# A layer on one core: from tile 4 on GpSimd makes the MLP's read instead of TensorE

## The chip, the cores and the metric

The kernel runs on one core of a Trainium2 chip. The time is the device time of one execution in microseconds; the number that counts is the median of the runs. All data is float32.

## The reference, cut to what matters

```python
def rat_read(res, W, gamma, beta, num_outputs):      # W is (512, outputs, 4)
    x = res.reshape(b, l, H, C)                      # H = 512, C = 4: 2048 values a row
    y = jnp.einsum('blhc,hoc->bloh', x, W)           # four neighbours make one value per output
    mu, var = y.mean(-1, keepdims=True), y.var(-1, keepdims=True)
    yn = (y - mu) * jax.lax.rsqrt(var + EPS)
    return (yn * gamma + beta).reshape(b, l, num_outputs * H)
...
qkv_in = rat_read(hidden_states, attn_read_w, ..., 3)
attn_out = attention(qkv_in, qkv_w, position_ids)            # causal, 16 heads
hidden_states = rat_write(hidden_states, attn_out, ...)      # the attention write
mlp_in = rat_read(hidden_states, mlp_read_w, ..., 2)         # the MLP's read
mlp_out = jax.nn.silu(gate(mlp_in[..., :H])) * up(mlp_in[..., H:])
hidden_states = rat_write(hidden_states, mlp_out, ...)       # the MLP write
...
x = x + layer(layernorm(x))
x = x + experts(layernorm(x))      # 8 experts of rank 16, weighed by a softmax router
```

`rat_write` makes from a projection of its input a new hidden state `hs * A_full + out * B_full`, elementwise over 2048 values a row, where `A_full` comes from exponentials of an outer product. x has 2 x 1024 rows of 2048 values.

## The kernel before

The 2048 rows are 16 tiles of 128 rows (one row a partition) and 4 blocks of 4 tiles. The program has three phases: the attention's reads and projections (`project_*`), the attention itself with the splitting of the MLP's weights on GpSimd (`attend_*`), and a mix of everything after (`mix_*`). Tiles 0 to 3 get their attention write partly during attention. All DMAs of the mix go out from one queue, SyncE's.

In the mix the work is made of small parts, each with a place on a common axis in which one MLP matmul step has length 1 and a block 64. The table `PLACES` gives the places: `a` is a tile's attention write and read, `w` its MLP write, `e` its expert, `t` the turn of a block, `h` the split of the MLP's middle, `m` the matmul steps. The list is sorted by place once, and each engine walks it in that order and does its share of each part; between engines only semaphores count. An engine never overtakes: what stands behind a waiting part waits too.

The parts of a tile `a`, i from 4 on, all on lane 0 (buffers `m_hs0`, `m_A0`): `load` of x into `m_hs0`, `wod` (16 matmuls, L1824), `low` and `delta` (L1838, L1845), `gates` (VectorE L1983 to L1998, among them the outer product L1992 into `m_A0`), `scale` (L2007, L2011, L2018, and on ScalarE L2213, L2217), `sum` (L2021, L2023, L2028, L2033, each over 1536 elements a partition). After the sum `m_hs0` holds the hidden state. Then comes the read: four `turn` parts, each with four 128x128 transposes on TensorE (L1809) and a copy from PSUM by ScalarE (L2183), and four `read` parts, each with four matmuls against `m_read2` (L1864; the profile has two records for each), which leave y in two PSUM banks. `stats` takes mean and variance on VectorE from PSUM (L2075, L2079, L2081) and a power on GpSimd (L2341); `norm` writes the normed y to `m_y0` to `m_y3` on ScalarE (L2241). The store of `m_hs0` to memory is issued by the queue at the place of `turn0`.

When a block's four tiles are there, the turn (`t`, TensorE L1908, VectorE L2130, ScalarE L2284, GpSimd L2353) makes the operand of its 32 matmul steps into the MLP (L1921, 12 matmuls each, a `m_win` weight load of 512 KB) and 32 steps out of it (L1933, `m_wods`, 316 KB). There are five weight buffers, and the load for step n + 5 is issued when step n is done. VectorE multiplies the middle (L2145) and splits it (L2159). The MLP write `w` of a tile runs the same instructions as `a` on lane 1 and ends with `x` (L2068, 2048 elements), on which the expert's first transpose (L1809 again) and its moments (ScalarE L2256, GpSimd L2347, L2349) wait. In blocks 1 and 2 the tiles `a` of the next block and `w` and `e` of the last one alternate.

In the profile, names stand without buffer numbers: `m_hs` is any of `m_hs0` to `m_hs2`.

## Time and profile before

| | |
|---|---|
| median of 3 runs | 1634.19 us (1629.28 to 1638.53) |
| profiled execution, span from first to last instruction | 1627.3 us |
| TensorE busy | 1531.8 us, 94% |
| VectorE busy | 1129.6 us, 69% |
| ScalarE busy | 921.9 us, 57% |
| GpSimd busy | 364.1 us, 22% |
| DMA queue of SyncE, share of 16 engines | 68.7% |
| blocks 0, 1, 2, 3 of the MLP | about 692 to 890, 894 to 1131, 1133 to 1358, 1359 to 1565 us |

Busy time is the time in which an engine runs at least one instruction. TensorE's groups share the time in which instructions overlap, so that a group's busy time is less than its count times its mean duration. For the profiled execution the page gives the span and no separate total; the median lies 6.9 us above the span.

### The profile page before, as it was taken

What the parts mean: (1) busy time and instruction counts of PE and PEld (TensorE: products, weight loads), DVE (VectorE), ACT (ScalarE), POOL (GpSimd) and SP (SyncE); (2) the same over time, 40 slices, a digit from 0 to 9 for tenths busy, and PEclk for the clock granted to TensorE, in tenths of its full rate; (3) what the DMA queues carried; (4) which work ended last, traced back from release to release, by engine and by line L of the source; (5) the groups of instructions that cost most, each with busy time, mean ns of one, the idle gap of its engine ahead of it and who ended that gap; (6) DMA issues with size and microseconds to landing.
All of it is one profiled execution on the core that took longest, in us unless ns stands there. A gap on an engine that the chain in (4) does not pass through costs nothing.

```text
span 1627.3 us, 25328 instructions
## 1 busy us (share of the span) xinstructions
PE 1531.8 (94%) x9574; PEld 1169.6 (72%) x9574; DVE 1129.6 (69%) x1782; ACT 921.9 (57%) x1702; POOL 364.1 (22%) x346
## 2 busy tenths in 40 slices
PE   7999999999999988899999999899999999999986
PEld 6567666666666656778798778798877898875554
DVE  7777745888888878644463785974776955636777
ACT  5444345888888776455543656643657644552443
POOL 1645555555433420110002000012000011001000
PEclk8999999999999999899999999999999999999998
DMA  9667677999987945356577766667766667756542
GB/s 371 204 254 243 223 181 229 276 293 284 273 233 197 253 138 189 130 185 223 202 218 233 258 226 221 214 218 232 265 233 221 223 197 237 218 180 213 203 178 104
DMA packets 127609, 360.94 MB, mean 222 GB/s; under 512 B 15744, under 2 KB 45056, under 8 KB 111872
## 3 DMA queue, kind: packets, MB, share of 16 engines
q1 hardware_dynamic: 127200, 359.19, 68.7%
q8 instruction: 76, 1.25, 0.3%
q14 instruction: 45, 0.37, 0.1%
q10 hardware_dynamic: 288, 0.13, 0.0%
HBM read 273.15 MB, written 86.11 MB: 221 GB/s over the span
## 4 chain that ended last, share of the span: by engine, by line
PE 74%; DVE 12%; ACT 6%; DMA 3%; issue 3%; POOL 1%; SPq 0%; DVEq 0%; ACTq 0%; POOLq 0%
PE ps L1921 21%; PE ps L1933 9%; PE ps L693 5%; PE ps L1249 5%; PE ps L1236 4%; PE ps L1272 4%; PE ps L1946 4%; PE ps L1879 3%; PE ps L1864 3%; PE ps L1809 3%; ACT a_p L1378 3%; PE ps L1824 3%; PE ps L1891 3%; DMA p_x<-in_x 2%; PE ps L652 2%
## 5 line engine op out<-in xcount | busy, mean ns | idle before, releaser
L1921 PE MATMUL ps<-m_y_split,m_win 128*128 128x512 f32 x1536 | 372.7, 396 | 2.7 <-issue 2.7
L1921 PEld LDWEIGHTS ps<-m_y_split,m_win 128*128 128x128 f32 x1536 | 284.2, 189 | 63.9 <-issue 7.1
L1308 DVE TENSOR_REDUCE a_negmax<-ps 128x1 f32<-128x640 f32 (+7 forms) x176 | 180.7, 1027 | 61.1 <-PE ps L1239 60.3
L1378 ACT ACTIVATE a_p<-ps,a_negmax 128x128 f32<-128x128 f32 (+7 forms) x256 | 188.5, 750 | 36.0 <-DVE a_negmax L1308 33.8
L1933 PE MATMUL ps<-m_wods,m_y_split 128*128 128x316 f32 x768 | 178.7, 322 | 3.8 <-DVE m_hT L2145 3.4
L2183 ACT ACTIVATE m_turned<-ps 128x512 f32<-128x512 f32 x128 | 75.0, 596 | 160.3 <-PE ps L1809 129.1
L1249 PE MATMUL ps<-ident,a_p 128*128 128x128 f32 x1152 | 157.8, 275 | 2.9 <-DVE a_pT L1321 2.0
L1236 PE MATMUL ps<-a_k,a_q 128*128 128x512 f32 (+3 forms) x384 | 124.4, 403 | 16.7 <-ACT a_p L1378 15.0
L1933 PEld LDWEIGHTS ps<-m_wods,m_y_split 128*128 128x128 f32 x768 | 128.5, 192 | 8.0 <-DVE m_hT L2145 3.7
L1249 PEld LDWEIGHTS ps<-ident,a_p 128*128 128x128 f32 x1152 | 123.5, 141 | 5.4 <-DVE a_pT L1321 3.5
L2341 POOL TENSOR_TENSOR m_scale<-m_scale,mhalf 128x2 f32<-128x2 f32 x16 | 13.0, 813 | 493.5 <-DVE m_scale L2081 493.5
L1933 PE MATMUL ps<-m_wods,m_hT_lo 128*128 128x316 f32 x384 | 118.8, 309 | 0.0
L1443 POOL TENSOR_SCALAR a_w_two<-a_w_raw 128x512 fp32r<-128x512 f32 (+1 forms) x64 | 79.8, 1247 | 155.5 <-DMA mlp_out_split<-a_w_two 72.0
L693 PE MATMUL ps<-p_yT,p_wqk 128*128 128x512 f32 x256 | 112.4, 594 | 1.0 <-ACT p_yvT L927 1.0
L2145 DVE TENSOR_TENSOR m_hT<-m_raw,ps 128x512 f32<-128x512 f32 x64 | 43.8, 685 | 97.6 <-PE ps L1921 97.4
L1321 DVE COPY a_pT<-ps 128x512 f32<-128x512 f32 (+3 forms) x190 | 108.1, 579 | 0.8 <-PE ps L1249 0.3
L1236 PEld LDWEIGHTS ps<-a_k,a_q 128*128 128x128 f32 x384 | 63.7, 192 | 54.9 <-ACT a_p L1378 30.8
L1392 ACT ACTIVATE a_pT<-ps 128x512 f32<-128x512 f32 (+3 forms) x154 | 82.8, 543 | 31.2 <-PE ps L1249 31.0
L693 PEld LDWEIGHTS ps<-p_yT,p_wqk 128*128 128x128 f32 x256 | 47.7, 190 | 57.4 <-issue 56.0
L939 ACT ACTIVATE p_rope_hi<-p_rope 128x512 fp32r<-128x512 f32 x32 | 20.1, 631 | 114.1 <-POOL p_rope L996 93.8
L2347 POOL TENSOR_SCALAR e_moments<-e_moments 128x1 f32<-128x1 f32 x16 | 10.6, 662 | 329.9 <-ACT m_x L2261 304.7
L1809 PE MATMUL ps<-ident,m_hs 128*128 128x128 f32 x464 | 70.1, 278 | 12.3 <-DVE m_hs L2068 4.7
(250 smaller groups left out, 3095.3 us busy)
## 6 DMA issues: line engine op xcount, KB each, us to landing
m_win<-mlp_in_split SPq DMA_DIRECT2D x128, 512.0 KB, 4.4
m_wods<-mlp_out_split SPq DMA_DIRECT2D x96, 316.0 KB, 3.3
p_xT<-in_xT SPq DMA_DIRECT2D x16, 1024.0 KB, 9.9
p_x<-in_x SPq DMA_DIRECT2D x16, 1024.0 KB, 10.6
a_q<-qk_split SPq DMA_DIRECT2D x64, 256.0 KB, 7.0
a_k<-qk_split SPq DMA_DIRECT2D x128, 128.0 KB, 7.2
mlp_in_split<-a_w_two SPq DMA_DIRECT2D x32, 512.0 KB, 5.5
m_hs<-in_x SPq DMA_DIRECT2D x15, 1024.0 KB, 5.6
```

Of the source, the lines that this page charges most:

```text
L693: m = nc.tensor.matmul(ps[:, b, :], wq[:, k, col:col + P], yT[:, k, :], start=(ic == 0), stop=(ic == HCH - 1))
L1236: nc.tensor.matmul(ps[:, bank + at, c0:c0 + kn], qs[s][:, qt * P:qt * P + P], ks[s][:, k0:k0 + kn], start=True, stop=k0 + kn < klen)
L1249: m = nc.tensor.transpose(ps[:, b, P * m_:P * m_ + P], src[:, j, P * k:P * k + P], ident[:, :])
L1308: V.tensor_reduce(negmax[:, n % 4, 0:len(units[n][3])], by_head(n, score_banks(n)), AX_X, ALU.max, negate=True).then_inc(max_ready, 1)
L1321: V.tensor_copy(kept[:, heads[j0]:heads[j1] + 1, k0:k1 + 1, P * q:P * q + P], ps[:, b, 0:P * len(part)].rearrange("p (a k b) -> p a k b", ...
L1378: m = S.activation(dst[:, j, :], src[:, j, :], ACT.Exp, bias=negmax[:, n % 4, j:j + 1], accum_out=rsum[:, si % 2, q * 4 + hh:q * 4 + hh + 1])
L1392: S.activation(kept[:, heads[j0]:heads[j1] + 1, k0:k1 + 1, P * q:P * q + P], ps[:, b, 0:P * len(part)].rearrange("p (a k b) -> p a k b", a ...
L1443: m = pool_own.then_inc(G.tensor_scalar(w_two[s][:, 0, 0:w], w_raw[r][:, 0:w], 1.0, None, ALU.mult))
L1809: m = nc.tensor.transpose(bank_of(what, i, "turn", q)[:, P * j:P * j + P], h[:, P * (4 * q + j):P * (4 * q + j) + P], ident[:, :])
L1921: m = nc.tensor.matmul(bank_of("m", blk, step), win[s][:, wl, ic, :], y[k], start=(ic == 0 and p3 == 0), stop=(ic == HCH - 1 and p3 == 2))
L1933: m = nc.tensor.matmul(bank_of("d", blk, q, r)[:, 0:HALFW], h[:, k, P * q:P * q + P], w2s[s][:, wl, :], start=(k == 0 and p3 == 0), stop=( ...
L2183: S.activation(tT[n % 2][:, :], bank_of(what, i, "turn", q), ACT.Copy).then_inc(one.sem((what, i, "turn", q)), 1)
```

## The change

From tile 4 on the parts `turn0` to `turn3` and `read0` to `read3` of `a` are gone, and four parts `fold0` to `fold3` stand at 10.1, 12.1, 14.1 and 16.1 behind the tile's base place. `fold` q runs on GpSimd: it multiplies 512 values of `m_hs0` by the read's weights of both outputs, which a DMA has repeated for all partitions (`m_read2_wide0` to `3`, 128x1024 each), into `m_A0`; a first addition folds four neighbours to two, a second folds two to one and writes 128 values of each output to the tile's `m_y` buffer. Each of the three waits for the one before it by a semaphore. `stats` then reads SBUF, in one instruction an output instead of two, and `norm` works in place, two ScalarE instructions instead of four. New waits: the first fold of a tile waits for the sum, for the wide weights, and for the turn of the block before (its `m_y`); VectorE's outer product into `m_A0` and the next load of `m_hs0` wait for the last fold of the tile before; `stats` waits for the tile's last fold. The store of `m_hs0` is issued at the place of `fold0`. Tiles 0 to 3 are as before. Three of the wide tables are loaded during attention; the fourth takes the room of `m_read2` and is loaded at the place of tile 4's `load`, when tile 3's read is over. To make room for the tables the program asks for a descriptor scratch of 1024 bytes (`dynamic_dma_scratch_size`).

```diff
@@ PLACES['A']
-       'turn0': 13.72,
-       'turn1': 14.22,
-       'read0': 15.22,
-       'read1': 15.23,
-       'turn2': 15.72,
-       'turn3': 16.91,
-       'read2': 17.94,
-       'read3': 17.95,
+       'fold0': 10.1,
+       'fold1': 12.1,
+       'fold2': 14.1,
+       'fold3': 16.1,
@@ write_step, "outer"
+                if lane_before[what, i] and lane_before[what, i][0] == "a":
+                    dve.wait_ge(folded, folds_of(lane_before[what, i][1]))
@@ write_dve
+            if part == "stats" and i >= TB:
+                c = i % TB
+                dve.wait_ge(folded, folds_of(i))
+                for o in range(RD2):
+                    n = dve_own.then_inc(V.bn_stats(m_st[:, c, o, 0, :], y2[c][:, o, :]))
...
@@ write_act, "norm"
+                if i >= TB:
+                    for o in range(RD2):
+                        m = S.activation(y2[c][:, o, :], y2[c][:, o, :], ACT.Identity, bias=m_sc[:, c, 2, o:o + 1],
+                                         scale=m_sc[:, c, 1, o:o + 1])
+                    m.then_inc(y2_ready, 1)
+                    return
@@ write_pool
+            if part == "fold":
+                c = i % TB
+                if q == 0:
+                    pool.wait_ge(hs_ready, nth("sum", what, i))
+                    pool.wait_ge(wide_loaded, 64)
+                    pool.wait_ge(turn2_mm, 8 * (i // TB))
+                x4 = hs[hs_of[what, i]][:, BLK * q:BLK * q + BLK].unsqueeze(1).broadcast_to([P, RD2, BLK])
+                prod, pairs = Ab[0][:, 0:RD2 * BLK], Ab[0][:, RD2 * BLK:RD2 * BLK + RD2 * P * 2]
+                p4 = prod.rearrange("p (g c) -> p g c", c=C)
+                p2 = pairs.rearrange("p (o h c) -> p o h c", o=RD2, c=2)
+                n = pool_own.then_inc(G.tensor_tensor(prod.rearrange("p (o f) -> p o f", o=RD2), x4,
+                                                      wide2[q][:, :, :], ALU.mult))
+                pool.wait_ge(pool_own.sem, n)
+                n = pool_own.then_inc(G.tensor_tensor(pairs.rearrange("p (g c) -> p g c", c=2), p4[:, :, 0:2],
+                                                      p4[:, :, 2:4], ALU.add))
+                pool.wait_ge(pool_own.sem, n)
+                G.tensor_tensor(y2[c][:, :, P * q:P * q + P], p2[:, :, :, 0], p2[:, :, :, 1], ALU.add).then_inc(folded, 1)
+                pool.wait_ge(folded, folds_of(i) - 3 + q)
@@ write_sp
             if part == "load":
+                if (what, i) == ("a", TB):
+                    for q2 in (2, 3):
+                        wait_for_quarter(sp, "a", TB - 1, q2)
+                    load_wide(0)
...
-                        sp.wait_ge(turnq_mm, quarter["a", j, 3] + 1)
+                        if j < TB:
+                            sp.wait_ge(turnq_mm, quarter["a", j, 3] + 1)
+                        else:
+                            sp.wait_ge(folded, folds_of(j))
...
-            if part == "turn" and q == 0:
+            if part in ("turn", "fold") and q == 0:
                 sp.wait_ge(hs_ready, nth("sum", what, i))
                 move(hs_d[i], hs[h][:, :]).then_inc(hs_stored[h], 16)
@@ kernel
-    nc = bacc.Bacc("TRN2", target_bir_lowering=False, num_devices=1)
+    nc = bacc.Bacc("TRN2", target_bir_lowering=False, num_devices=1, dynamic_dma_scratch_size=1024)
```

How the order of instructions moves is shown at three places. In the changed kernel the line numbers are higher: L1824 is L1839 there, L1809 is L1824, L1838 is L1853, L1845 is L1860, L1921 is L1936, L2341 is L2391, L2347 and L2349 are L2397 and L2399, L2353 is L2403; L2380, L2383 and L2386 are the three instructions of a fold. The number behind a name is a buffer's.

TensorE at the read of tile 8, early in block 1, before:

```order
L1921 MATMUL ps<-m_y_split_217,m_win3_145 128x512 x12
L1809 MATMUL ps<-ident_49,m_hs0_180 128x128 x8
L1921 MATMUL ps<-m_y_split_217,m_win4_150 128x512 x12
L1864 MATMUL ps<-m_read2_155,m_turned0_205 128x64 x4
L1864 MATMUL ps<-m_read2_155,m_turned1_206 128x64 x4
L1838 MATMUL ps<-ident_49,m_att_ab_177 32x128 x4
L1921 MATMUL ps<-m_y_split_217,m_win0_136 128x512 x12
L1809 MATMUL ps<-ident_49,m_hs0_180 128x128 x4
L1921 MATMUL ps<-m_y_split_217,m_win1_139 128x512 x12
L1809 MATMUL ps<-ident_49,m_hs0_180 128x128 x4
L1845 MATMUL ps<-m_duT0_161,m_lowT0_162 128x512
```

The same place in the changed kernel, to the expert's first transpose of tile 0 (`m_hs1`):

```order
L1936 MATMUL ps<-m_y_split_221,m_win3_145 128x512 x12
L1936 MATMUL ps<-m_y_split_221,m_win4_150 128x512 x12
L1853 MATMUL ps<-ident_49,m_att_ab_177 32x128 x4
L1936 MATMUL ps<-m_y_split_221,m_win0_136 128x512 x12
L1936 MATMUL ps<-m_y_split_221,m_win1_139 128x512 x12
L1860 MATMUL ps<-m_duT0_161,m_lowT0_162 128x512
L1936 MATMUL ps<-m_y_split_221,m_win2_142 128x512 x12
L1936 MATMUL ps<-m_y_split_221,m_win3_145 128x512 x12
L1824 MATMUL ps<-ident_49,m_hs1_185 128x128 x4
```

All transposes of `m_hs0` and all matmuls with `m_read2` are gone from between the matmul steps; the rest stands in the same order.

GpSimd between the turn of block 1 and the expert of tile 0, before:

```order
L2353 TENSOR_TENSOR m_y_split_217<-m_raw0_207,m_y_split_217 128x512
L2353 TENSOR_TENSOR m_y_split_217<-m_raw1_208,m_y_split_217 128x512
L2341 TENSOR_TENSOR m_scale_179<-m_scale_179,mhalf_50 128x2
L2347 TENSOR_SCALAR e_moments0_170<-e_moments0_170 128x1
L2349 TENSOR_TENSOR e_moments0_170<-e_moments0_170,mhalf_50 128x1
```

And in the changed kernel (the second quarter of the fold and the third stand between, alike):

```order
L2403 TENSOR_TENSOR m_y_split_221<-m_raw1_212,m_y_split_221 128x512
L2380 TENSOR_TENSOR m_A0_188<-m_hs0_184,m_read2_wide0_180 128x1024
L2383 TENSOR_TENSOR m_A0_188<-m_A0_188 128x512
L2386 TENSOR_TENSOR m_y0_194<-m_A0_188 128x2x128
...
L2380 TENSOR_TENSOR m_A0_188<-m_hs0_184,m_read2_wide3_183 128x1024
L2383 TENSOR_TENSOR m_A0_188<-m_A0_188 128x512
L2386 TENSOR_TENSOR m_y0_194<-m_A0_188 128x2x128
L2391 TENSOR_TENSOR m_scale_179<-m_scale_179,mhalf_50 128x2
L2397 TENSOR_SCALAR e_moments0_170<-e_moments0_170 128x1
```

Twelve instructions a tile stand ahead of the tile's power and of the expert's two small ones.

The queue of SyncE at the store of tile 5 and the load of tile 6, before:

```order
L301 DMA m_wod1_140<-in_wod1T 128x632
L301 DMA m_wod2_143<-in_wod1T 128x632
L301 DMA m_wod3_146<-in_wod1T 128x632
L301 DMA m_wod4_151<-in_wod1T 128x632
...
L301 DMA m_win0_136<-mlp_in_split 128x1024
L301 DMA hidden_after_attention<-m_hs0_180 128x2048
L301 DMA m_win1_139<-mlp_in_split 128x1024
L301 DMA m_win2_142<-mlp_in_split 128x1024
L301 DMA m_win3_145<-mlp_in_split 128x1024
L301 DMA m_hs0_180<-in_x 128x2048
```

And in the changed kernel, where the load of tile 6 follows eleven places behind the store:

```order
L297 DMA m_win0_136<-mlp_in_split 128x1024
L297 DMA m_wod1_140<-in_wod1T 128x632
L297 DMA m_wod2_143<-in_wod1T 128x632
L297 DMA m_wod3_146<-in_wod1T 128x632
L297 DMA hidden_after_attention<-m_hs0_184 128x2048
L297 DMA m_wod4_151<-in_wod1T 128x632
L297 DMA m_win0_136<-mlp_in_split 128x1024
L297 DMA m_win1_139<-mlp_in_split 128x1024
```

The store, which waits for the tile's sum, stands seven loads earlier.

## Rows read from the trace of the kernel before

**Rows 1.** Stretches: start:end, length, busy us of PE, PEld, DVE, ACT, POOL, clock, DMA

```profile
700.00:872.00 172.00, 167.81 (x933) 143.47 (x933) 82.06 (x126) 84.17 (x124) 4.34 (x6) 0.98 0.67 215
872.00:1100.00 228.00, 219.05 (x1303) 185.38 (x1303) 163.55 (x234) 132.88 (x212) 20.66 (x20) 0.99 0.68 230
1100.00:1335.00 235.00, 228.31 (x1342) 190.48 (x1342) 166.01 (x244) 131.15 (x213) 18.62 (x18) 1.00 0.69 231
...
1015.30:1052.00 36.70, 32.55 (x183) 26.43 (x183) 33.69 (x53) 21.23 (x43) 0.70 (x1) 0.91 0.60 199
```

**Rows 2.** Groups by line, TensorE: count, busy us, mean ns, idle before, releasers

```profile
L1809 PE MATMUL ps<-ident,m_hs 128*128 128x128 f32 x464 | 70.1, 278 | 12.3 <-DVE m_hs L2068 4.7 <-DVE m_lowT L2053 3.8 <-ACT m_att_out L2224 2.2
...
L1864 PE MATMUL ps<-m_read,m_turned 128*128 128x64 f32 x512 | 62.0, 272 | 3.9 <-ACT m_turned L2183 3.5 <-issue 0.3
```

**Rows 3.** Groups by line, GpSimd, two-input operations of two sizes

```profile
L1445 POOL TENSOR_TENSOR a_w_two<-a_w_raw,a_w_two 128x512 fp32r<-128x512 f32 x32 | 40.9, 1278 | 2.7
...
L1445 POOL TENSOR_TENSOR a_w_two<-a_w_raw,a_w_two 128x316 fp32r<-128x316 f32 x32 | 27.5, 859 | 2.7
```

**Rows 4.** Timeline (start us, us), VectorE beside GpSimd; durations of L779 min/median/max ns

```profile
888.28 1.29 POOL L2353 TENSOR_TENSOR m_y_split<-m_raw,m_y_split 128x512 fp32r<-128x512 f32 x1 [1.16 <-ACT m_y_split L2284]
...
888.74 1.38 DVE L1983 TENSOR_TENSOR m_delta<-m_delta,m_tmp 128x512 f32<-128x512 f32 x1
...
L779 DVE TENSOR_TENSOR nmr<-rstd,p_negmean x16: 147/153/1268, 18.3 to 212.9; 128x1 f32<-128x1 f32 x16
...
1500.55 2.58 POOL L2347 TENSOR_SCALAR e_moments<-e_moments 128x1 f32<-128x1 f32 x1 [50.88 <-ACT m_x L2261]
...
1501.33 1.75 DVE L2023 SCALAR_TENSOR_TENSOR m_A<-m_A,m_gate 128x1536 f32<-128x1536 f32 x1
```

**Rows 5.** Timeline, VectorE behind tile 11's sum; then its `m_A` instructions in a stretch

```profile
1066.15 0.68 DVE L1983 TENSOR_TENSOR m_delta<-m_delta,m_tmp 128x512 f32<-128x512 f32 x1
...
1080.57 2.29 DVE L2068 TENSOR_TENSOR m_hs<-m_hs,m_x 128x2048 f32<-128x2048 f32 x1
...
1064.50:1082.90 18.40, 10.42 (x6) 1.00 0.65 222
```

**Rows 6.** Timeline, L2068 and the expert's first transpose, tiles 0 and 1

```profile
925.92 2.28 DVE L2068 TENSOR_TENSOR m_hs<-m_hs,m_x 128x2048 f32<-128x2048 f32 x1
...
930.45 0.61 PE L1809 MATMUL ps<-ident,m_hs 128*128 128x128 f32 x4
...
968.75 2.29 DVE L2068 TENSOR_TENSOR m_hs<-m_hs,m_x 128x2048 f32<-128x2048 f32 x1
...
992.88 0.60 PE L1809 MATMUL ps<-ident,m_hs 128*128 128x128 f32 x4
```

**Rows 7.** Timeline of block 0: sums of tiles 4, 5, 7, splits, loads, norm, turn

```profile
723.69 1.76 DVE L2033 TENSOR_TENSOR m_hs<-m_hs,m_A 128x1536 f32<-128x1536 f32 x1
...
745.05 0.36 SPq L301 DMA_DIRECT2D m_hs<-in_x  x1
...
770.36 1.76 DVE L2033 TENSOR_TENSOR m_hs<-m_hs,m_A 128x1536 f32<-128x1536 f32 x1
...
816.69 3.69 DVE L2159 TENSOR_TENSOR m_hT_lo<-m_hT,m_y_split 128x512 fp32r<-128x512 f32 x6
...
833.76 0.38 SPq L301 DMA_DIRECT2D m_hs<-in_x  x1
...
848.66 1.76 DVE L2033 TENSOR_TENSOR m_hs<-m_hs,m_A 128x1536 f32<-128x1536 f32 x1
...
867.19 1.93 ACT L2241 ACTIVATE m_y<-ps,m_scale 128x256 f32<-128x256 f32 x4 [5.16 <-DVE m_scale L2085]
...
872.56 0.60 PE L1908 MATMUL ps<-ident,m_y 128*128 128x128 f32 x4
```

**Rows 8.** One matmul step in the chain of waits; weight load: KB, us to landing

```profile
741.81 2.78 PE ps L1921 x12
...
m_win<-mlp_in_split SPq DMA_DIRECT2D x128, 512.0 KB, 4.4
```

More of the change, by code:

```diff
@@ L262, in program @@
             read1_in, gamma1_in, beta1_in, qkvT, wod1T, wab1_b, du1_rows,
-            read2_in, gamma2_in, beta2_in, mlp_inT, wod2T, wab2_b, du2_rows,
+            read2_in, read2_rows, gamma2_in, beta2_in, mlp_inT, wod2T, wab2_b, du2_rows,
             expA, expB, br, out):
@@ L418, in program @@
         place[0] = ring_end
+        read2_place = place[0]
         read2 = sb("m_read2", [P, DCH, RD2, HPC])
+        read2_end = place[0]
         gam2 = sb("m_gamma2", [P, RD2 * HCH])
@@ L445, in program @@
         m_sc = sb("m_scale", [P, TB, 3, RD2])
+        wide2 = []
+        after, place[0] = place[0], read2_place
+        wide2.append(sb("m_read2_wide0", [P, RD2, BLK]))
+        assert place[0] == read2_end
+        place[0] = after
+        wide2 += [sb(f"m_read2_wide{q}", [P, RD2, BLK]) for q in (1, 2, 3)]
         place[0] = keep
@@ L585, in program @@
             sem(n) for n in ("y2_ready", "turn2_mm", "yhi_ready", "ylo_ready"))
+        wide_loaded, folded = sem("wide_loaded"), sem("folded")
         wt_loaded = sems("wt_loaded", NW)
@@ L1563, in prepare_sp, with load_wide @@
             load_du(0)
+            for q in (1, 2, 3):
+                load_wide(q)
+        def load_wide(q):
+            move(wide2[q][:, :, :], read2_rows[q].unsqueeze(0).broadcast_to([P, RD2, BLK])).then_inc(wide_loaded, 16)
         def load_du(k):
@@ L1656, in nth, with folds_of @@
             return number[part, what, i]
+        def folds_of(i):
+            return 4 * (i - TB + 1) if i >= TB else 0
         def nth_before(part, what, i):
@@ L2068, in write_dve @@
                 V.tensor_tensor(hs[h][:, :], hs[h][:, :], m_x[x_at][:, :], ALU.add).then_inc(x2_ready, 1)
-            if part == "stats":
+            if part == "stats" and i >= TB:
[3 more added lines that the diff above has]
+                    n = dve_own.then_inc(V.bn_stats(m_st[:, c, o, 0, :], y2[c][:, o, :]))
+                dve.wait_ge(dve_own.sem, n)
+                for o in range(RD2):
+                    n = dve_own.then_inc(V.bn_aggr(m_my[:, c, o, :], m_st[:, c, o, 0, :]))
+                dve.wait_ge(dve_own.sem, n)
+                V.tensor_scalar(m_sc[:, c, 0, :], m_my[:, c, :, 1], EPS, None, ALU.add).then_inc(yvar2_ready, 1)
+            if part == "stats" and i < TB:
                 c = i % TB
@@ L2236, in write_act @@
                 act.wait_ge(yscale2_ready, i + 1)
-                act.wait_ge(turn2_mm, 8 * (i // TB))
+                if i >= TB:
+                    for o in range(RD2):
+                        m = S.activation(y2[c][:, o, :], y2[c][:, o, :], ACT.Identity, bias=m_sc[:, c, 2, o:o + 1],
+                                         scale=m_sc[:, c, 1, o:o + 1])
+                    m.then_inc(y2_ready, 1)
+                    return
                 for a in range(2):
@@ L2529 @@
         "read2": read_rep(L0_xattn_mlp_read_w, RD2),
+        "read2_rows": lay(np.transpose(np.reshape(L0_xattn_mlp_read_w, (4, P, RD2, C)), (0, 2, 1, 3)).reshape(4, RD2, BLK)),
         "gamma2": lay(np.reshape(L0_xattn_mlp_read_g, (RD2 * HCH, P)).T),
```

## The prediction

> **What bounds the kernel now.** The first view to read is the table of stretches [rows 1]. From 700 to 1335 us the kernel works through three blocks of the MLP, and there TensorE is busy 167.8 of 172, 219.1 of 228 and 228.3 of 235 us. GpSimd is busy 4 to 21 us of each. So TensorE's own work sets the pace, at a granted clock of 0.98 to 1.00 of the 2.4 GHz level, and GpSimd is nearly free. The reader should also see VectorE's column: 82 us of 172 in the first block, but 164 of 228 and 166 of 235 in the next two, because there each attention write (a tile's `a` part) is followed by an MLP write and an expert part. In one stretch of block 1, from 1015 to 1052 us, VectorE is busy 33.7 of 36.7 us and TensorE only 32.6, with its clock at 0.91: VectorE leads there already.
>
> **What is removed.** For each of 12 tiles TensorE loses 16 transposes and the read's 32 matmul records. Per instruction the groups' busy time counts, not the mean duration, since instructions overlap: 70.1 us / 464 = 0.151 us and 62.0 / 512 = 0.121 us [rows 2]. 16 x 0.151 + 32 x 0.121 = 6.3 us a tile, 75.5 us in all. That is the whole of what can be won, and it would come out in full if nothing else came last. ScalarE loses four copies of a turned quarter, and its four pieces of the norm become two; VectorE's four statistics become two. ScalarE is busy 133 of 228 us in block 1, so its own idle time hides these edits; they cost and bring nothing.
>
> **What is added, in GpSimd's own time.** A fold of a quarter is a product of 1024 elements a partition, a sum of 512 and a sum of 256. GpSimd's two-input operations took 1278 ns at 512 and 859 ns at 316 elements [rows 3]: 2.14 ns an element and 0.18 us fixed. So 2.37 + 1.28 + 0.73 = 4.4 us, with three waits on its own semaphore of some 0.09 us each 4.65 us, and 18.6 us for a tile. Nothing in the trace shows the strided or repeated operands; dense rows are the nearest, so 18.6 is the value and the bottom, and the top I take a third higher, 25 us. The Trainium skill (GPSIMD Engine Reference, 3.1 Elementwise) has 4497 ns for a two-input sum of 2048 elements; by it a tile would be an estimated 16 us of elements and the fixed parts. No row here has that size.
>
> **What it collides with.** This is the step that decides. At 888.28 GpSimd started a two-input operation of 1.29 us; at 888.74 VectorE started L1983, which takes 0.68 us elsewhere [rows 5], and it took 1.38, until 0.55 us behind GpSimd's end. L779, on one element, has a median of 153 ns and a longest of 1268 ns, under a GpSimd operation. The other way round, GpSimd's one-element operation at 1500.55 took 2.58 us and ended when VectorE's L2023 ended (1501.33 + 1.75) [rows 4]. So a VectorE instruction with two inputs in SBUF and a GpSimd operation that reads SBUF do not run side by side: the later one stands still. The Trainium skill has the same as a rule (SBUF — State Buffer, Who interferes with whom): such a pair shares one read interface, held for the whole instruction. It speaks against this change, and the trace agrees. Were there no such hold, the sum below would be the first rival's.
>
> Where does a fold fall? It starts when the tile's sum (L2033) ends. In blocks 1 and 2 VectorE goes straight into the MLP write of another tile. From the start of L1983 at 1066.15, where the sum ended, to the end of L2068 at 1082.9 it spent 10.4 us on `m_A` instructions, 2.3 on L2068 and 0.7 on L1983; with L2007, L2011 and L2018 between them some 15.5 to 16 of 16.7 us are in the form that cannot run beside the fold [rows 5]. The eight such tiles look alike. VectorE's ten larger instructions there each find a GpSimd operation in front of them. A mean operation is 4.4 / 3 = 1.46 us, so at most 10 x 1.46 = 14.6 us is inserted, and if each is met at half its length, 7.3. I take 12, with 8 and 16 as ends, as the queue of GpSimd is never empty during a fold.
>
> **Blocks 1 and 2, tile by tile.** TensorE's next need of VectorE is the expert's first transpose, which waits for L2068. It started 2.2 us behind it at 930.45, and 21.8 us behind it at 992.88 [rows 6], the least and the most of eight; the eight gaps are 2.2, 21.8, 8.5, 3.2, 10.6, 18, 5.3 and 10.1. The removed work lies between the write's start and this transpose, so TensorE gets there 6.3 us sooner, and VectorE 12 us later. The transpose moves by the larger of -6.3 and 12 less the gap: +9.8, -6.3, +3.5, +8.8, +1.4, -6.3, +6.7, +1.9, together **+20 us**. With 8 us inserted the same sum is -5, with 16 it is +48. The covers that are gone are named by it: the transposes and reads were what TensorE did while VectorE finished.
>
> **Block 0.** No MLP write runs there, so the folds of tiles 4, 5 and 7 meet little. Here a chain decides: `m_hs0` and `m_A0` serve every such tile, so the load of the next tile, the queue's and the outer product on VectorE wait for the last fold. Tile 4's sum ends at 725.45; with the fold 744.2, and the next load, issued at 745.05 before, goes at about 744. Tile 5's sum ended at 772.1, now about 766 as TensorE is ahead; fold until 785; tile 6's sum at 805 instead of 816.7, where the splits began. Behind it VectorE has the splits (L2159, six in 3.7 us and more after), two-input instructions all; nine of them add some 6 to 9 us, so the fold ends near 831. The load of tile 7 goes out then, where it was at 833.76; from load to the end of the sum took 16.7 us (850.4), so 848; fold 867, and about 5 us of statistics, power and norm (the four norm pieces took 1.93): 872. TensorE's turn of this block began at 872.56 [rows 7]. So the 25 us that four tiles save in block 0 are given back at the turn: **0 us**, from -8 (the splits pass between the operations) to +6.
>
> **Other edits.** The store of `m_hs` moves from the first transpose's place to the first fold's, past the four `m_wod` and several `m_win` loads of the queue. It waits for the sum, with the weight loads behind it. Five weight buffers are ahead, 5 x 2.78 us of matmul steps [rows 8], and I cost it at 0, up to 5 us if that cover is gone. The three wide loads (1.5 MB) go out during attention, where TensorE waits for no DMA: 0 to +1. The fourth follows the last read. The smaller descriptor scratch only gives room: 0. Block 3 has no folds: 0.
>
> Sum: 20 + 0 + 0 = +20 us. The sum is made on the execution with a span of 1627.3 us; the median of the runs, 1634.19, lies 6.9 above it, an offset that I keep. **1654 us.**
>
> **The rivals.** *The fold is hidden.* GpSimd is idle over 90% of these blocks, so that 4 x 18.6 us a block fit, and if VectorE's gaps take the held instructions, TensorE's 75.5 us come out, less block 0's chain of 25: 1634 - 50 = 1584. For it: TensorE is above 95% busy and hardly waits. Against it: [rows 4] and the gap of 2.2 us. 12%. *Half and half.* About 8 us or a little less is inserted: -5 in blocks 1 and 2, up to -8 in block 0, 1621 to 1634. 18% within 0.5%, 10% below that. *The other side, further out: the weight queue runs dry.* The next tile's load waits for all four quarters of the fold, in the one queue that also brings the weights. With folds of 30 us beside VectorE's work the queue stands some 10 to 17 us at tiles 7, 11, 13 and 15. From the point where that is more than five steps less a landing (13.9 - 4.4 = 9.5 us [rows 8], less in the shorter steps), TensorE starves. Some 7 us at four places, 1654 + 28 = 1682. 10%. *The fold is a third longer than dense rows say:* four times 6.3 us on block 0's chain, 1679. 6%. The forecast itself has 44%.
>
> The chances: slower 44 + 10 + 6 = 60%, within 0.5% (8.2 us, about what a measurement of this kernel can tell from no change) 18%, faster 12 + 10 = 22%. The range runs from 1605, inside the first rival, to 1685, which takes in the last two.
>
> **What would show it.** L1983, L2007, L2021 and L2068 get longer durations while GpSimd folds, and a fold takes about 19 us in block 0 at tiles 4, 5 and 7 but about 30 in blocks 1 and 2. TensorE's busy time drops by about 75 us, and idle time before L1809 (the expert's, now another line number) and L1908, for VectorE and ScalarE, comes in its place. The turn of block 1 begins near 872 us, as before, though 25 us of work in front of it are gone. The prediction is wrong if VectorE's two-input instructions keep their length, if TensorE's idle time grows by less than 60 us, or if its new idle time stands behind weight loads.

## The result: 4.5% slower, where 1.2% was forecast

The changed kernel took 1707.95 us (median of 4 runs, 1706.2 to 1709.85) against 1636.36 us for the kernel before on the same chip, a ratio of 1.0455 with a 95% interval of 1.0431 to 1.048. The forecast was 1654, from 1605 to 1685: the direction came, the size did not (+72 us instead of +20), and the time lies outside the range.

The page of the changed kernel (busy us and share of the span; then the granted TensorE clock in 40 slices, 9 for 90% or more; then the chain by engine):

```profile
span 1706.0 us, 24177 instructions
...
PE 1514.6 (89%) x8998; PEld 1141.2 (67%) x8998; DVE 1225.2 (72%) x1758; ACT 891.2 (52%) x1630; POOL 597.5 (35%) x490
...
PEclk8999999999999999899799998989889779999998
...
PE 54%; DVE 28%; ACT 7%; issue 5%; DMA 3%; POOL 2%; SPq 0%; DVEq 0%; ACTq 0%; POOLq 0%
```

TensorE has 576 instructions fewer but only 17 us less of busy time, 1514.6 against 1531.8. VectorE has 24 instructions fewer and 96 us more. Its share of the chain rose from 12% to 28%.

The stretches between the turns of the blocks, as in [rows 1]: start:end, length, busy us of TensorE, weight loads, VectorE, ScalarE, GpSimd, granted clock, DMA share. The cuts are the starts of the first transposes of `m_y`.

```profile
688.87:881.90 193.03, 170.41 (x805) 139.42 (x805) 99.83 (x128) 78.93 (x109) 80.89 (x60) 0.91 0.61 201
881.90:1141.51 259.61, 213.97 (x1099) 175.64 (x1100) 202.40 (x225) 122.77 (x187) 100.70 (x68) 0.89 0.57 198
1141.51:1413.40 271.89, 223.94 (x1154) 182.69 (x1153) 211.41 (x236) 121.54 (x189) 105.39 (x66) 0.89 0.58 200
1413.40:1706.00 292.60, 266.71 (x1359) 195.72 (x1356) 178.53 (x250) 131.75 (x215) 22.23 (x26) 0.98 0.55 189
```

The same four stretches were 187.3, 226.7, 235.5 and 292.6 us before, with TensorE busy 181.8, 217.7, 228.8 and 266.8 and a granted clock of 0.96, 0.98, 1.00 in the first three. So the block without folds is unchanged, the first has lost 5.7 us, and the next two 32.9 and 36.4. In the first three TensorE's idle time grew from 21.2 to 116.2 us, and its busy time fell by 20.0 only. The rest of the difference between the two spans, 3.6 us, lies ahead of the first turn (685.26 and 688.87 us); the kernel before with nothing but the smaller scratch has it at 691.33, so this is scatter.

What TensorE waited for (us in total, times, longest):

```profile
PE ps L1901 <- DVE e_weighted L2140: 43.0, 6, 9.9
PE ps L1860 <- DVE m_lowT L2070: 22.6, 7, 8.2
PE ps L1839 <- DMA m_wod<-in_wod1T: 20.3, 6, 5.8
PE ps L1948 <- DVE m_hT L2172: 17.0, 3, 9.9
...
PE ps L1824 <- DVE m_hs L2085: 8.7, 2, 4.7
```

Only the last is the wait that the forecast priced, and 4.7 of its 8.7 us were there before. The largest one (10.5 us before), L1901, transposes the expert's weighted low projection; the third stands behind weight loads.

### The profile page after: what moved, and what is told of

The parts are those of the page before. It is cut to its first block, busy times and chain, and to the rows that moved or that the text cites. A ratio compares the mean times of both kernels' runs of the same rounds, so it can differ in the third digit from the quotient of the medians.

```text
span 1706.0 us, 24177 instructions
## 1 busy us (share of the span) xinstructions
PE 1514.6 (89%) x8998; PEld 1141.2 (67%) x8998; DVE 1225.2 (72%) x1758; ACT 891.2 (52%) x1630; POOL 597.5 (35%) x490
## 4 chain that ended last, share of the span: by engine, by line
PE 54%; DVE 28%; ACT 7%; issue 5%; DMA 3%; POOL 2%; SPq 0%; DVEq 0%; ACTq 0%; POOLq 0%
PE ps L1936 13%; PE ps L1948 5%; PE ps L699 5%; PE ps L1255 5%; PE ps L1242 4%; PE ps L1278 4%; PE ps L1961 4%; ACT a_p L1384 3%; DVE m_A L2040 2%; DVE m_A L2045 2%; PE ps L1906 2%; DVE m_A L2009 2%; DVE m_hs L2038 2%; PE ps L658 2%; PE ps L1894 2%
## 5 line engine op out<-in xcount | busy, mean ns | idle before, releaser
L1936 PE MATMUL ps<-m_y_split,m_win 128*128 128x512 f32 x1536 | 382.3, 406 | 2.9 <-issue 2.7
L1936 PEld LDWEIGHTS ps<-m_y_split,m_win 128*128 128x128 f32 x1536 | 296.0, 195 | 70.0 <-issue 8.4
L1948 PE MATMUL ps<-m_wods,m_y_split 128*128 128x316 f32 x768 | 192.9, 342 | 26.4 <-DVE m_hT L2172 17.0
L2380 POOL TENSOR_TENSOR m_A<-m_hs,m_read_wide 128x1024 f32<-128x1024 f32 x48 | 124.3, 2590 | 139.3 <-DVE m_hs L2050 136.5
L1948 PEld LDWEIGHTS ps<-m_wods,m_y_split 128*128 128x128 f32 x768 | 141.5, 210 | 34.0 <-DVE m_hT L2172 17.8
L1449 POOL TENSOR_SCALAR a_w_two<-a_w_raw 128x512 fp32r<-128x512 f32 (+1 forms) x64 | 80.1, 1252 | 159.0 <-DMA mlp_out_split<-a_w_two 75.5
L2397 POOL TENSOR_SCALAR e_moments<-e_moments 128x1 f32<-128x1 f32 x16 | 9.0, 564 | 334.9 <-ACT m_x L2293 309.8
L1948 PE MATMUL ps<-m_wods,m_hT_lo 128*128 128x316 f32 x384 | 125.8, 328 | 0.0
L2210 ACT ACTIVATE m_turned<-ps 128x512 f32<-128x512 f32 x80 | 46.7, 593 | 79.3 <-PE ps L1824 47.9
L1839 PE MATMUL ps<-m_wod,m_oT 128*128 128x512 f32 x192 | 63.5, 484 | 20.5 <-DMA m_wod<-in_wod1T 20.3
L1948 PEld LDWEIGHTS ps<-m_wods,m_hT_lo 128*128 128x128 f32 x384 | 80.3, 209 | 0.0
```

The lines of the kernel that those rows point to most:

```text
L1449: m = pool_own.then_inc(G.tensor_scalar(w_two[s][:, 0, 0:w], w_raw[r][:, 0:w], 1.0, None, ALU.mult))
L1936: m = nc.tensor.matmul(bank_of("m", blk, step), win[s][:, wl, ic, :], y[k], start=(ic == 0 and p3 == 0), stop=(ic == HCH - 1 and p3 == 2))
L1948: m = nc.tensor.matmul(bank_of("d", blk, q, r)[:, 0:HALFW], h[:, k, P * q:P * q + P], w2s[s][:, wl, :], start=(k == 0 and p3 == 0), stop=( ...
L2380: n = pool_own.then_inc(G.tensor_tensor(prod.rearrange("p (o f) -> p o f", o=RD2), x4, wide2[q][:, :, :], ALU.mult))
```

## What a fold does to VectorE

The timeline of the changed kernel at tile 8, GpSimd (start us, us) and then VectorE:

```profile
926.25 2.94 POOL L2380 TENSOR_TENSOR m_A<-m_hs,m_read_wide 128x1024 f32<-128x1024 f32 x1
929.26 1.04 POOL L2383 TENSOR_TENSOR m_A<-m_A 128x512 f32<-128x512 f32 x1
930.38 2.01 POOL L2386 TENSOR_TENSOR m_y<-m_A 128x256 f32<-128x256 f32 x1
...
926.24 0.68 DVE L1998 TENSOR_TENSOR m_delta<-m_delta,m_tmp 128x512 f32<-128x512 f32 x1
926.84 2.41 DVE L2000 SCALAR_TENSOR_TENSOR m_gate<-m_mlp_ab,m_gate 128x48 f32<-128x48 f32 x1
929.28 2.63 DVE L2009 TENSOR_TENSOR m_A<-m_delta,m_gate 128x1536 f32<-128x1536 f32 x1
```

VectorE's L2000, 48 elements and 0.20 us before, took 2.41: it ends at 929.25, the product on GpSimd at 929.19. L2009 starts 0.02 us behind GpSimd's L2383, which ends at 930.30, and ends 1.6 us later (it takes 1.76 us alone). GpSimd in turn took 2.01 us for 256 elements that take 0.61 alone, until 0.5 us behind L2009's end. They alternate; neither runs beside the other. The hold of L2009 is what the forecast described, but it had counted "ten larger instructions": the small ones are held too, for up to twelve times their length. By form, means in ns of before and after: `m_gate` of 48 elements 203 and 985, `e_weighted` 352 and 861, `m_hT_lo` 686 and 1021.

Where this reaches TensorE, at tile 11:

```profile
1105.74 0.31 PE L1948 MATMUL ps<-m_wods,m_hT_lo 128*128 128x316 f32 x1
1115.93 0.47 PE L1901 MATMUL ps<-ident,e_weighted 128*128 128x128 f32 x1 [9.88 <-DVE e_weighted L2140]
1116.05 0.88 PE L1948 MATMUL ps<-m_wods,m_y_split 128*128 128x316 f32 x2
...
1113.38 2.34 POOL L2380 TENSOR_TENSOR m_A<-m_hs,m_read_wide 128x1024 f32<-128x1024 f32 x1
...
1108.42 2.71 DVE L2028 TENSOR_TENSOR m_tmp<-m_tmp,m_mlp_out 128x512 f32<-128x512 f32 x1
...
1113.37 2.50 DVE L2140 SCALAR_TENSOR_TENSOR e_weighted<-e_low,e_moments,e_router 128x128 f32<-128x128 f32 x1
...
1116.00:1122.00 6.00, 6.00 (x21) 4.97 (x22) 5.97 (x3) 1.58 (x4) 4.45 (x2) 0.55 0.19 57
```

The small instruction that makes `e_weighted` stands in VectorE's queue behind held ones and is held itself (2.50 for 0.35 us). TensorE stands for 9.88 us with the MLP's matmuls, which need nothing of it, behind a transpose of 0.47 us. And the next 6 us run at a granted clock of 0.55, close to the 1.2 GHz level: two matmuls that took 0.45 us in front of the wait take 0.88 behind it. So a wait costs more than its own length.

## Experiments

Each run is given as median and ratio to the kernel before on the same chip, with its 95% interval.

### Which part costs: the reads, the length of the folds, or the place of the store

**e1_tiny.** All waits and places stay, but the folds work on few elements: the MLP's read is left out. **e2_memset** replaces the fold by memsets of about its length, which read nothing (the read is left out too).

The product in e1 (the two sums are cut alike), and then what stands for all three in e2:

```diff
-                n = pool_own.then_inc(G.tensor_tensor(prod.rearrange("p (o f) -> p o f", o=RD2), x4,
-                                                      wide2[q][:, :, :], ALU.mult))
+                n = pool_own.then_inc(G.tensor_tensor(prod.rearrange("p (o f) -> p o f", o=RD2)[:, :, 0:4], x4[:, :, 0:4],
+                                                      wide2[q][:, :, 0:4], ALU.mult))
```
```diff
+                for width in (1536, 1000, 1400, 400):
+                    n = pool_own.then_inc(G.memset(Ab[0][:, 0:width], 1.0))
+                    pool.wait_ge(pool_own.sem, n)
+                G.memset(y2[c][:, :, P * q:P * q + P], 1.0).then_inc(folded, 1)
```

> The changed kernel with every fold cut to a few elements: GpSimd's three instructions a quarter, all semaphores, all loads and the store's new place stay, the arithmetic of the fold is left out. If the 72 us that the change costs come from the fold's length or from what it holds back on VectorE, the 75.5 us of TensorE work that are gone come out nearly whole: 1565 to 1580 us. If they come from what stays (the store that waits for the sum in the queue of weight loads, the wide loads, the smaller scratch), it stays above 1620 us. I expect 1575.

> The changed kernel with the folds replaced by memsets on GpSimd of about the same total length (4.3 us a quarter, nothing read from SBUF), with all waits kept; the fold's arithmetic is left out. Theory 1 (a GpSimd operation that reads SBUF holds VectorE's two-input instructions): VectorE is no longer held, L1998 to L2085 keep their length of before, and most of the loss goes, 1580 to 1610 us. Theory 2 (the latency of the fold in the chain of waits for m_hs0, m_A0 and the statistics): it stays at 1690 to 1710 us. I expect 1595, with block 0 still near 187 us because its chain is latency.

Measured 1628.53 (0.9961, 0.9943 to 0.998) and 1634.26 (0.9997, 0.9977 to 1.0017). Both missed, by 53 and 39 us: the reads' 74 us were there (1707.95 - 1634.26), but the gain of the removed work was not. Something else eats it, and the trace of e1 points at it:

```profile
PE ps L1839 <- DMA m_wod<-in_wod1T: 21.7, 6, 5.8
...
720.11 3.05 SPq L297 DMA_DIRECT2D m_wod<-in_wod1T  x2
730.82 0.33 SPq L297 DMA_DIRECT2D hidden_after_attention<-m_hs  x1
731.19 1.40 SPq L297 DMA_DIRECT2D m_wod<-in_wod1T  x2
```

The queue stands at the store until the sum is there, and two `m_wod` loads leave 8 us after the end of the two in front of them.

**e3_store** is the changed kernel with the store back at 13.72, **e9_tiny_store** is e1 with it, **e18_memset_store** is e2 with it, and **e16_store_early** is the kernel before with nothing but the store at 10.1.

```diff
+       'keep0': 13.72,
-            if part in ("turn", "fold") and q == 0:
+            if (part == "keep" or (part == "turn" and i < TB)) and q == 0:
```

> The changed kernel with the store of m_hs0 at its old place, 13.72 instead of 10.1 behind the tile's base. The queue of loads waited 79 us for the sum between 689 and 1413 us where it did not before, and TensorE then waited 20 us in all for loads of m_wod. If that queue wait costs time of its own, this gives 1685 to 1695 us and TensorE's waits for m_wod go; if VectorE was late anyway it stays within 5 us of the changed kernel's 1708. I expect 1695.

> The kernel of e1_tiny (folds of a few elements, arithmetic left out) with the store of m_hs0 back at 13.72. In e1_tiny 75.5 us of TensorE work were gone and the time fell by 6.7 us. Theory A (the store's early place makes the queue of weight loads wait for the sum, TensorE waits for m_wod, and its clock falls after each wait): block 0 falls from 190.8 to about 175 us, and the run to 1605 to 1612. Theory B (VectorE's and ScalarE's parts are late in the rearranged order whatever the queue does): block 0 stays above 185 us and the run at 1622 to 1628. I expect 1608, by A in block 0 and B in the blocks 1 and 2.

> The kernel before, complete, with the store of m_hs0 at 10.1 instead of 13.72 and nothing else. With tiny folds the early store cost 40.6 us (1628.5 against 1587.9), with full folds 16.5. Theory A: the queue waits for the sum with the weight loads behind it, whatever else is changed: 15 to 40 us slower, with waits of TensorE for m_wod. Theory B: it costs only where TensorE has become faster than VectorE: 0 to 8 us. I expect 12 us, 1646.

> The changed kernel with the store at 13.72 and memsets of the fold's length instead of the folds (arithmetic left out): the fold's latency and all its waits without its reads. Between e9_tiny_store (1587.9, no latency) and e3_store (1691.5, latency and reads). The prediction gave back 25 us of block 0 to the chain by latency. If latency costs there, block 0 takes 172 to 179 us instead of 163.6 and the run 1597 to 1606; if only the reads cost, it is 1588 to 1592. I expect 1600.

| | store early | store at 13.72 |
|---|---|---|
| folds read (changed kernel, e3) | 1707.95 | 1691.45 (1.0351, 1.0319 to 1.0382) |
| memsets of their length (e2, e18) | 1634.26 | 1609.26 (0.9838, 0.9805 to 0.9871) |
| tiny folds (e1, e9) | 1628.53 | 1587.88 (0.9707, 0.968 to 0.9734) |
| no folds, TensorE's read (e16, before) | 1670.61 (1.0216, 1.0195 to 1.0237) | 1635.72 |

The runs stand on several chips, on which the kernel before took 1633.56 to 1636.36 us; differences between rows are good to some 3 us. e3 came as expected. e9 was expected at 1608 and is 20 us faster, e18 at 1600 and is 9 slower, and e16 at 1646 and is 25 slower: for e9 and e16 I had set the store's price too low.

The place of one DMA costs 16.5 to 40.6 us, 35 alone (1670.61 - 1635.72). With folds in place it costs the more the shorter they are: 16.5, 25.0 and 40.6 us. In e16 the waits behind it are the same ones:

```profile
PE ps L1825 <- DMA m_wod<-in_wod1T: 21.8, 6, 5.8
...
SPq L302 <- DVE m_hs L2034: 100.7, 14, 19.7
```

The second row is the queue's own wait for the sum, 14 times, up to 19.7 us. In the kernel before this wait comes twice, and not once between 688 and 1335 us, since there the sum is done at the store's place:

```profile
SPq L301 <- DVE m_hs L2033: 19.9, 2, 19.1
```

The right column splits the rest. From 1634, removing TensorE's read brings 46 us (1588; the forecast's sum had 75.5). That GpSimd is occupied for 17 us a tile, while the statistics, the next load and the next outer product wait for it, costs 21 (1609). That the folds read SBUF costs 82 (1691), the largest term, and the early store 16.5 (1708).

**e4_scratch** is the kernel before with the smaller descriptor scratch alone.

> The kernel before with the smaller descriptor scratch alone (1024 bytes). All theories expect no change, 1634 to 1638 us. If the scratch matters for the queue's loads, it is slower by some us; the changed kernel reached the turn of block 0 at 688.9 instead of 685.3 us.

1635.15 (1.0001, 0.9986 to 1.0015): no effect.

### The hold by itself

Here GpSimd does extra work in the kernel before, for which nobody waits: **e5_reads** runs the fold's three instructions on dummy buffers for 12 tiles, **e6_writes** memsets instead.

```diff
+       'fold0': 10.1,
...
+            if part == "fold":
+                if q == 0:
+                    pool.wait_ge(hs_ready, nth("sum", what, i))
+                n = pool_own.then_inc(G.tensor_tensor(prod.rearrange("p (o f) -> p o f", o=RD2), x4,
+                                                      dum[1][:, :].rearrange("p (o f) -> p o f", o=RD2), ALU.mult))
...
```

In e6 these lines stand for the three instructions:

```diff
+                for k, width in ((2, 1024), (1, 1024), (2, 900), (1, 900), (2, 600)):
+                    n = pool_own.then_inc(G.memset(dum[k][:, 0:width], 1.0))
+                    pool.wait_ge(pool_own.sem, n)
```

> The kernel before, complete, with an added load on GpSimd: from the end of each of the 12 sums it runs the fold's three instructions a quarter, same shapes, on tables of its own, and nobody waits for them; the smaller scratch gives the room. Theory 1 (a GpSimd operation that reads SBUF holds VectorE's two-input instructions): VectorE's busy time grows by 80 to 100 us, and the time by 60 to 80 us, to 1695 to 1715, nearly all of it in blocks 1 and 2. Theory 2 (the loss is of the new waits): within 5 us of 1635. I expect 1700.

> As e5_reads, but with memsets of about the same total length (some 4.3 us a quarter), which write SBUF and read nothing. Theory 1 gives no change, 1633 to 1640 us; if any work on GpSimd disturbs VectorE or the time comes from the expert's small GpSimd operations standing behind the added ones, it is like e5_reads or over 1645. I expect 1637.

e5 took 1722.09 (1.0528, 1.0501 to 1.0556), 22 us above what was expected, e6 1635.45 (1.0007, 0.9994 to 1.002), as expected. The added work keeps GpSimd busy for 243 us in e5, where it is itself held, and for 203 in e6, and VectorE's busy time differs by 94 us:

```profile
PE 1563.7 (91%) x9574; PEld 1194.3 (69%) x9574; DVE 1230.2 (72%) x1782; ACT 922.2 (54%) x1702; POOL 606.7 (35%) x493
```
```profile
PE 1539.1 (94%) x9574; PEld 1173.2 (72%) x9574; DVE 1136.6 (69%) x1782; ACT 921.6 (56%) x1702; POOL 566.8 (35%) x589
```

One more reading has to go: GpSimd's small instructions, for which VectorE does wait, stand behind the added work, and that work is longer in e5. Their wait is the same in both, first e5 and then e6:

```profile
DVE m_scale L2090 <- POOL m_scale L2362: 8.5, 8, 2.4
...
DVE m_scale L2090 <- POOL m_scale L2352: 8.4, 8, 2.3
```

So GpSimd's reading alone, without any wait on it, costs 88 us, and its occupation at this place nothing. The Trainium skill (SBUF — State Buffer, Who interferes with whom) says that a VectorE instruction with two SBUF inputs contends with a GpSimd instruction that reads SBUF, and not with one that only writes it; both runs agree.

### Does the gap ahead of the expert's transpose cover the hold?

The forecast's step was: a tile costs 12 less its gap [rows 6], and nothing where the gap is larger. **e13_reads_9_13** gives dummy reads to two tiles with large gaps (21.8 and 18 us), **e14_reads_8_11** to two with small ones (2.2 and 3.2; `i in (8, 11)`). Both against e5:

```diff
-            if part == "fold":
+            if part == "fold" and i in (9, 13):
```

> The kernel before, complete, with the added GpSimd reads of e5_reads behind the sums of tiles 9 and 13 only. The prediction let the gap between L2068 and the expert's first transpose (21.8 and 18 us there) take the 12 us that VectorE is held. If that step is right: 0 us, 1633 to 1637. If the hold comes out nearly whole because TensorE needs VectorE at other places first (the transposed low part, the bank of the middle, the weighted low part): e5_reads lost 83.8 us in eight tiles of blocks 1 and 2, so two of them lose some 20 us, 1650 to 1658. I expect 1650.

> As e13_reads_9_13, but behind the sums of tiles 8 and 11, where the gaps are 2.2 and 3.2 us. By the prediction's step +9.8 and +8.8 less what is won nowhere here, so 12 + 12 - 5.4 = 18.6 us: 1654. By the other reading the same 20 us as for tiles 9 and 13. The two together tell whether the gap matters: if it does, this is some 18 us slower than e13_reads_9_13, else they are alike within 6. I expect 1655.

1653.51 (1.011, 1.0089 to 1.0132) and 1653.2 (1.0112, 1.0093 to 1.0131): 8.9 and 8.7 us a tile. For the small gaps the step comes out (9.8 + 8.8 = 18.6, measured 17.5), as it would for any rule that lets the hold through; for the large ones it is wrong (0, measured 17.8). With large gaps the held time comes out elsewhere; of e13, the waits from 870 to 1400 us, and tile 13 in the timeline:

```profile
PE ps L1814 <- ACT m_att_out L2229: 5.3, 2, 4.6
PE ps L1814 <- DVE m_att_ab L2049: 4.2, 2, 3.6
...
PE ps L1891 <- DVE e_weighted L2118: 3.4, 1, 3.4
...
1215.37 1.09 PE L1814 MATMUL ps<-ident,m_hs 128*128 128x128 f32 x4 [4.61 <-ACT m_att_out L2229]
1225.09 1.11 PE L1814 MATMUL ps<-ident,m_hs 128*128 128x128 f32 x4 [3.62 <-DVE m_att_ab L2049]
```

None of these three is in the same stretch of the kernel before with more than 1.5 us. And the four transposes behind each wait took 1.1 us where [rows 6] has 0.60: the granted clock was 0.50, the 1.2 GHz level, from 1215 to 1221 us, and 0.74 from 1225 to 1231.

### Does another place for the reads help?

**e17_reads_behind_x** lets the dummy reads of tiles 8 to 15 begin behind the MLP write's sum with x. **e19_writes_behind_x** has the same places with memsets. **e20_reads_last** puts the reads behind the tile's power on GpSimd and ahead of the expert's two small instructions. The places of e17 and e19, and then e20's against them:

```diff
+                    if part[:4] == "fold" and i >= 2 * TB:
+                        placed.append((PLACES["w"][i - 2 * TB] + 6.8 + 0.01 * q, (what, i, "fold", q)))
+                        continue
```
```diff
-                        placed.append((PLACES["w"][i - 2 * TB] + 6.8 + 0.01 * q, (what, i, "fold", q)))
+                        at = max(PLACES["a"][i] + 17.96, PLACES["e"][i - 2 * TB] + 8.68)
+                        placed.append((at + 0.01 * (q + 1), (what, i, "fold", q)))
```

> The kernel before, complete, with the added GpSimd reads of e5_reads (12 tiles, same operations), but for tiles 8 to 15 they begin only when the MLP write that follows the sum is over (behind L2068 and not behind the sum). If the loss is VectorE held inside its dense run of two-input instructions, most of the 83.8 us of the blocks 1 and 2 in e5_reads goes: 1645 to 1665 us, with VectorE's busy time up by 20 to 50 instead of 100 us. If the mere amount of reading on GpSimd costs, it stays at 1700 to 1722. I expect 1660.

1708.33 (1.0438, 1.0401 to 1.0475), a miss of 48 us. VectorE's busy time had grown by 31 us only, so I formed a second theory, a queue on GpSimd.

> The run before it with GpSimd reading dummies behind the MLP write's sum with x (tiles 8 to 15) cost 73 us although VectorE's busy time grew by only 31 us instead of 101. Two readings. Queue reading: GpSimd's small power for a tile's scale and the expert's moments stand behind the moved block of 17 us, and VectorE, which never overtakes, waits for them (69 us of such waits in that run). Reading by reads: it is the reads themselves, wherever they stand. This run has the same places and the same waits, but GpSimd fills the time with memsets, which read nothing. The queue reading expects 1690 or more (nearly all of the 73 us). The reads reading expects within 5 us of the kernel before. I expect the queue reading, 1692.

> Kernel before plus the same dummy reads of GpSimd for 12 tiles (nobody waits for them), but for tiles 8 to 15 they stand behind the tile's small power and only the expert's moments of the same pair of tiles come behind them. So neither the MLP write's two-input instructions nor the tile's scale meets them. If the place of the reads decides what the hold costs, the run should lie far under the 1722 of the same reads started at the sum: VectorE's busy time grows by 40 us or less and the time is 1650 to 1665. If the amount of reading costs wherever it falls, it is 1700 or more. I expect 1660: some 9 us in the first block and some 2 us a tile for expert moments that come up to 5 us late.

e19: 1702.46 (1.042, 1.039 to 1.0451). e20: 1677.48 (1.0259, 1.0244 to 1.0275). Nearly the same cost, 68 of 74 us, comes without a single read, so in e17 it was the queue. VectorE's waits in e17 and in e19:

```profile
DVE m_scale L2093 <- POOL m_scale L2367: 69.3, 14, 14.2
```
```profile
DVE m_scale L2093 <- POOL m_scale L2357: 84.4, 14, 15.8
```

A power of 2 elements stands behind 17 us of GpSimd work, VectorE waits for it, and all of VectorE's queue behind that. (Before, this wait is 6.5 us in total.) In e20 this wait is 7.4 us, and the reads cost 43 us, half of e5's 88 for the same amount, with VectorE 61 us busier instead of 101. The place of the reads thus decides about half of the price, and none that I tried brings it near zero; e20 lies above the 1650 to 1665 that I had given for a harmless place. How much of the 43 is still queue is open: the expert's two small instructions and the turn's `m_y_split` stand behind the reads there (VectorE's wait for the latter is 10.3 us instead of 4.6), and memsets in e20's place were not run.

### Fewer folds

**e10_block0** has folds only for tiles 4 to 7, **e12_457** only for 4, 5 and 7, leaving out tile 6, whose fold runs beside VectorE's splits; both with the store at 13.72 and TensorE's read elsewhere, and with a still smaller scratch (128 bytes).

```diff
+FOLD = (4, 5, 7)
...
+       'turn0': 13.72,
...
+                    if what == "a" and part[:4] in (("turn", "read") if i in FOLD else ("fold",)):
+                        continue
```

> Folds on GpSimd for tiles 4 to 7 only, the read on TensorE as before for tiles 8 to 15, and the store of m_hs0 at its old place for all; the fourth wide table has a place of its own (scratch of 128 bytes). In e3_store block 0 took 179.4 us against 187.3 before, with the blocks 1 and 2 losing 65. If the loss is VectorE's held instructions in the MLP writes of blocks 1 and 2, this version has block 0 at 179 and the others as before: 1625 to 1629 us, faster than the kernel before. I expect 1627.

> As e10_block0, but with folds for tiles 4, 5 and 7 only; tile 6, whose fold runs beside VectorE's splits (L2159) and behind which block 0 stood 16.5 us idle, is read by TensorE. Against e10_block0 (block 0 178.9 us, 1629 us): 6.3 us of TensorE work more, and the 10 us less in the chain from tile 6 to tile 7 if the held splits are what block 0 lacks (with tiny folds it took 163.6). Then block 0 takes 173 to 176 us and the run 1622 to 1626; if it is the fold's latency, it is 180 us and 1630. I expect 1624.

1629.18 (0.9971, 0.9953 to 0.9988) and 1626.52 (0.9941, 0.9922 to 0.996). The latter is the fastest kernel here that computes the whole layer, 0.6% under the kernel before. Its stretch of block 0 is 176.6 us instead of 187.3, and 178.9 in e10. That lies between the two readings which e12 was to tell apart, so whether the rest of block 0's loss is tile 6's held splits or the fold's latency stays open.

## Why the prediction was wrong, point by point

**Blocks 1 and 2 (+20): the step that failed, +69.** Of the 69 us, 4 are the store's: with the store at its old place (e3) the two blocks take 527.7 us against 462.1 before, +66. The size of the hold is not what was wrong. VectorE is busier by 10.8, 39.0 and 45.3 us in the three stretches, so 2.7 us a tile in block 0 and about 10.5 later, where 12 (8 to 16) was forecast; with 10.5 the forecast's own sum of max(-6.3, 12 - gap) would give +10. What failed is the sum, in both of its terms:

- *The gap as a cover.* It took the expert's first transpose as the only place where TensorE meets VectorE. e13 against e14 shows that a gap there covers nothing: there are five kinds of such places (`m_lowT`, `m_att_ab`, `m_hT`, `m_hs`, `e_weighted`), VectorE is busy 7 of 10 us, and what it loses in one place is late at the next. From memsets to reads (e18 to e3) VectorE is 84 us busier in the two blocks, and they take 80 us longer.
- *The removed work, 6.3 us a tile.* With nothing else late (e9) block 0 became 23.7 us shorter, near the 25 of the sum, but the blocks 1 and 2 only 20 us, where 50 were due. TensorE's busy time fell by 23, 19 and 17 us there, and its idle time in the blocks 1 and 2 rose from 15.6 to 31.2: the removed transposes and reads had filled time in which TensorE otherwise waits. Why its busy time fell by less than 25 a block is not shown.

**The removed work in all (75.5 us): mis-sized.** In e9 46 us came out of the time and 59 of TensorE's busy time in the three stretches. In the changed kernel TensorE's busy time fell by 20 only.

**The clock: missing from the sum.** e9 and the changed kernel give TensorE the same instructions. Its busy time in the three stretches is 569 us in one and 608 in the other; of e9:

```profile
692.00:856.00 164.00, 158.50 (x803) 131.68 (x804) 88.14 (x128) 79.64 (x111) 24.57 (x60) 0.97 0.70 232
856.00:1072.00 216.00, 198.78 (x1098) 164.62 (x1097) 162.03 (x225) 122.58 (x187) 36.35 (x68) 0.98 0.71 240
1072.00:1298.00 226.00, 212.06 (x1157) 173.30 (x1156) 165.17 (x236) 121.12 (x189) 38.75 (x66) 0.98 0.72 241
```

The 39 us more go with a granted clock of 0.89 to 0.91 instead of 0.97 to 0.98, and with 80 us more of idle time. For every 2 us of waiting about 1 us was lost again by slower matmuls. The forecast priced a wait at its own length. [Rows 1] had a warning, a clock of 0.91 in the stretch in which VectorE led.

**The length of a fold: right in block 0.** 2590, 1281 and 1019 ns are the three means, 611 the least of the last; a tile's fold took 16.9, 16.9, 20.6 and 17.0 us in block 0 (forecast 18.6, called the bottom) and 19.2 to 24.3 later (forecast about 30).

**The store (0, up to 5): wrong.** It costs 16.5 us here and 35 alone. The cover that was named is five weight buffers, each a full `m_win` step long. But directly behind seven of the twelve stores now stand one to three of the next tile's four `m_wod` loads, and these are not that far ahead. In the kernel before, those of tile 5 are issued from 714.77 to 723.26, take 2.9 us to land, and their matmuls begin at 725.46:

```profile
714.77 8.49 SPq L301 DMA_DIRECT2D m_wod<-in_wod1T  x4
...
725.46 4.48 PE L1824 MATMUL ps<-m_wod,m_oT 128*128 128x512 f32 x16
```

In the changed kernel TensorE waits 20.3 us in all for them, 12.3 of it in block 0, and in e3, with the store back, not at all. This was one of the forecast's own signs of being wrong, new idle time behind weight loads.

**Block 0 (0, -8 to +6): +5.7, in the range by luck.** The chain of one `m_hs0` and one `m_A0` is there, but smaller than forecast: with folds and the store at its old place, e3 has 179.4 us, tiny folds 163.6 (e9), memsets of a fold's length 178.0 (e18). So 24 us are saved, and 14 given back by GpSimd's occupation, 1 by the reads and 14 by the store. The forecast had 25 saved and all 25 given back by the chain; two errors, -8 and +14, nearly cancel.

**The rivals.** *The weight queue runs dry* came true in another form: the loads of the next tile do not matter, the store in front of the weights does. *The fold is hidden* is excluded by e5. Scratch 0, block 3 at 0: right.

## What to carry to other kernels

Before moving work to GpSimd, count what it reads from SBUF: in this kernel the two-input VectorE instructions beside it wait for it, the small ones for many times their own length, so a GpSimd that is idle for 78% of the time isn't free. Count too what then stands behind it in its own queue. Where TensorE waits for VectorE at many places, price an inserted microsecond at nearly a microsecond (from 0.8 in e13 to 0.95 between e18 and e3, the clock's share included), and don't set one gap against it. Before a DMA with a wait is moved forward in a queue, read the lead of every load that then stands behind it.

## What the hardware showed that I had not expected

- A VectorE instruction of 48 elements (0.20 us) takes up to 2.41 us beside a GpSimd product of 1024.
- Memsets that keep GpSimd busy for 35% of the span instead of 22% cost 0.07% (-0.06% to 0.2%); reads of about the same length cost 5.3%.
- From 949 to 956 us, behind a wait of 4.0 us, the granted clock was 0.63; behind one of 9.9 us, from 1116 to 1122 us, 0.55. A matmul step of twelve took 4.96 us instead of 2.9:

```profile
949.18 1.11 PE L1824 MATMUL ps<-ident,m_hs 128*128 128x128 f32 x4 [3.99 <-DVE m_hs L2085]
949.95 4.96 PE L1936 MATMUL ps<-m_y_split,m_win 128*128 128x512 f32 x12
...
949.00:956.00 7.00, 6.82 (x24) 5.64 (x25) 2.50 (x8) 5.61 (x8) 0.71 (x1) 0.63 0.04 5
```
